# A four-layer graph network on one core: weights loaded by SP in the order of use, and the order of steps rearranged

## The chip, the cores and the metric

The kernel runs on one core of a Trainium2 chip. The metric is the device time of one execution in microseconds (us). Three runs of the kernel before are at hand, and one more execution that the hardware profiler recorded; all rows below come from that one.

## What is computed

64 independent graphs, each with 128 nodes and 384 features, pass through four stages, and each stage is added to the stream x of features:

```python
h = relu(layernorm(x)); x = x + L0(h, adj)   # "a": 2 layers; softmax(h h^T) * adj, three weights (left, self, right)
h = relu(layernorm(x)); x = x + L1(h, adj)   # "b": 2 layers; bilinear scores with two weights, one linear weight
h = relu(layernorm(x)); x = x + L2(h, adj)   # "c", layer 0: 12 heads, Wq, Wk, Wv, Wo
h = relu(layernorm(x)); x = x + L3(h, adj)   # "c", layer 1: 12 heads, Wq, Wk, Wv
```

There are 3 + 3 + 3 + 3 + 4 + 3 = 19 weights of 384 x 384, all used by every graph.

## The kernel before

**Numbers.** Products with weights run in float16 on TensorE (PE). Each weight is kept as two halves: `w_hi`, the weight times 64 rounded to float16, and `w_lo`, what the rounding lost. Activations are split the same way. A weight arrives in one of four stage buffers (`w_stage`: two of its own, and the still unused tiles `score` and `prob`), ScalarE (ACT) writes its upper half (`split_high`, L668), then VectorE (DVE) its lower half (`split_low`, L966; in a trace it shows under its helper's line L699). A stage buffer is free again when the lower half is written (`w_lo_split`).

**Order.** Every engine executes its instructions in the order written. That order is made by `woven`: the work of a graph is cut into steps, a letter stands for a stream of steps, and the string `ORDER[engine]` is one period. In each period each letter takes its stream one step on; `FIRST` says in which period and at which occurrence a stream begins. So graph g's stage a runs beside stage b of graph g - 1 and stage c of g - 2 and g - 3, and a steady period handles one graph's worth of everything. On PE: `a` turns the node features (transposes through the unit matrix), makes the scores of stage a (called U here), turns the attention, and makes the context (ctx); `w` are its weight products, each in two steps, called hl, hr and hs here; `d` turns the adjacency (L391, one instruction in each period, a handy mark); `b` and `x` are the same for stage b; `c` and `y` for stage c, whose turned features wait in bank c0, v product in c1, q and k in c2 and c3.

**Weights in the first periods.** SP loads the first four weights, after x and adj of two graphs and beta. The split of the first three weights stands ahead of everything else on ACT and DVE. The other 16 are put between steps at the places of `SPLITS` (period, place). Their loads are issued by ACT inside `split_high`: ahead of splitting weight m it waits for `w_lo_split` to reach m, and issues the load of weight m + 3. ACT also issues the two small copies that put the bias halves into `bias_hl`. POOL (GpSimd) begins with the memset of `bias_hl` (L1034) and then makes the constants; later it computes the inverse roots (`rstd`, L992). SP issues x and adj of graph g once `x1` of graph g - 2 is there (`load`).

**Names in the rows.** `node_a`, `node_b`, `node_c`: normalized features, whose turning on PE (L328) begins a layer; `hta_hi`, `hta_lo`: turned features of stage a; `sides`: copies of hl and hr; `self_part`: copy of hs times the diagonal of the attention; `ctx_a` (L766) adds it; `x1` is written at L792, x2 at L868 and L947.

## Time and profile before

| | us |
|---|---|
| median of 3 runs | 3139.33 |
| lowest and highest | 3137.36, 3139.83 |
| the profiled execution, its own time | 3139.59 |
| its span, first to last instruction | 3137.8 |
| busy in the span: PE, PE's weight loads (PEld) | 3032.1 (97%), 2337.5 (74%) |
| busy: DVE, ACT, POOL | 2606.3 (83%), 2094.4 (67%), 377.2 (12%) |
| granted PE clock, mean | 0.984 |

1.8 us of the profiled execution lie outside the span. A PE matmul is shown with its full latency, and the next one begins inside it, so the distance between two starts tells the pace, and a short pause can hide in a busy figure. Matmuls are counted as busy on PE, loading of the stationary operand on PEld. PEclk is the granted clock as a share of 2.4 GHz. "<-" behind an idle time names what ended it.

### The profile page before, as it was taken

Reading aid. Unit: us, or ns where it says so; the run is one execution under the profiler, and the core shown is the slowest. Engines: PE = TensorE matmul, PEld = TensorE weight load, DVE = VectorE, ACT = ScalarE, POOL = GpSimd, SP = SyncE. Lnnn points to the kernel's source line nnn. Section 1 sums busy time; section 2 is a strip of 40 time slices with the busy share of each in tenths; the row PEclk is TensorE's granted clock in tenths of the full one; section 3 lists DMA queues with packets and bytes.
Section 4 is the critical chain, followed back from the end, with each engine's and each line's share of the span. In section 5 each row is a group of like instructions: output and inputs, shape, how many; then the busy total and the mean of one; then the engine's idle time right before and its main releaser. Section 6 shows DMA issues by size and latency. Waiting matters only on the chain. (4 is left out here: it accounts for less than half of the span.)

```text
span 3137.8 us, 87682 instructions
## 1 busy us (share of the span) xinstructions
PE 3032.1 (97%) x34944; PEld 2337.5 (74%) x34944; DVE 2606.3 (83%) x7641; ACT 2094.4 (67%) x6037; POOL 377.2 (12%) x652
## 2 busy tenths in 40 slices
PE   3899999999999999999999999999999999999986
PEld 1677777777777777777777777777777777777764
DVE  4688888888888888888888888888888888888874
ACT  4467677677677677677676676676676666666664
POOL 1111111111111111111111111111111111111100
PEclk7999999999999999999999999999999999999996
DMA  5000000000000000000000000000000000000000
GB/s 174 4 14 11 10 13 11 12 12 11 13 10 11 13 10 11 13 10 11 13 10 11 14 10 11 13 10 11 14 10 11 13 10 11 14 10 11 10 7 6
DMA packets 37904, 47.82 MB, mean 15 GB/s; under 512 B 4542, under 2 KB 37498, under 8 KB 37498
## 3 DMA queue, kind: packets, MB, share of 16 engines
q1 hardware_dynamic: 31408, 33.31, 3.4%
q10 hardware_dynamic: 6090, 8.91, 0.9%
q8 instruction: 278, 4.55, 0.6%
q14 instruction: 128, 1.05, 0.1%
HBM read 29.59 MB, written 12.58 MB: 13 GB/s over the span
## 5 line engine op out<-in xcount | busy, mean ns | idle before, releaser
L638 ACT ACTIVATE prob<-score,neg_head_max 128x128 f32<-128x128 f32 x1536 | 494.1, 392 | 117.5 <-DVE neg_head_max L901 117.2
L284 PE MATMUL bank_c<-htc_hi,w_hi 128*128 128x128 f16 x2304 | 397.2, 220 | 0.0
L284 PE MATMUL bank_c<-htc_lo,w_hi 128*128 128x128 f16 x2304 | 397.1, 219 | 0.0
L284 PE MATMUL bank_c<-htc_hi,w_lo 128*128 128x128 f16 x2304 | 397.0, 219 | 0.0
L284 PE MATMUL bank_a<-w_hi,hta_hi 128*128 128x384 f16 x1152 | 379.6, 330 | 0.0
L284 PE MATMUL bank_a<-w_lo,hta_hi 128*128 128x384 f16 x1152 | 378.8, 329 | 0.0
L699 DVE SCALAR_TENSOR_TENSOR pt_lo<-bank_c,pt_hi 128x384 f16<-128x384 f32 x512 | 271.1, 550 | 74.3 <-ACT pt_hi L518 70.1
L896 DVE SCALAR_TENSOR_TENSOR score<-bank_c,bias 128x384 f32<-128x384 f32 x512 | 281.0, 549 | 33.7 <-PE bank_c L459 29.8
L901 DVE TENSOR_REDUCE neg_head_max<-score 128x3 f32<-128x384 f32 x512 | 280.4, 548 | 6.8
L518 ACT ACTIVATE pt_hi<-bank_c 128x384 f16<-128x384 f32 x512 | 233.0, 481 | 63.5 <-PE bank_c L328 63.5
L328 PE MATMUL bank_c<-ident,prob 128*128 128x128 f32 x1536 | 257.8, 278 | 14.1 <-ACT prob L638 13.7
L284 PE MATMUL bank_a<-w_hi,hta_lo 128*128 128x384 f16 x1152 | 252.5, 329 | 0.0
L328 PEld LDWEIGHTS bank_c<-ident,prob 128*128 128x128 f32 x1536 | 189.6, 143 | 75.7 <-issue 22.3
L284 PEld LDWEIGHTS bank_c<-htc_lo,w_hi 128*128 128x128 f16 x2304 | 226.0, 98 | 9.3 <-issue 0.3
L284 PEld LDWEIGHTS bank_c<-htc_hi,w_hi 128*128 128x128 f16 x2304 | 226.0, 98 | 8.6 <-issue 0.5
L284 PEld LDWEIGHTS bank_c<-htc_hi,w_lo 128*128 128x128 f16 x2304 | 225.9, 98 | 0.0
L518 ACT ACTIVATE m_hi<-bank_b 128x384 f16<-128x384 f32 x256 | 125.1, 489 | 142.3 <-PE bank_b L322 126.7
L284 PE MATMUL bank_b<-htb_lo,w_hi 128*128 128x128 f16 x1152 | 209.4, 219 | 0.0
L284 PE MATMUL bank_b<-htb_hi,w_hi 128*128 128x128 f16 x1152 | 209.4, 219 | 0.0
L284 PE MATMUL bank_b<-htb_hi,w_lo 128*128 128x128 f16 x1152 | 209.4, 219 | 0.0
L284 PE MATMUL bank_a<-sides,attn_ta 128*128 128x384 f32 x512 | 188.1, 490 | 2.8 <-DVE attn_ta L753 2.6
L284 PE MATMUL bank_c<-w_lo,htc_hi 128*128 128x384 f16 x576 | 190.0, 331 | 0.0
(200 smaller groups left out, 9183.0 us busy)
## 6 DMA issues: line engine op xcount, KB each, us to landing
x_in<-x SPq DMA_DIRECT2D x64, 192.0 KB, 2.4
out<-y_out SPq DMA_DIRECT2D x64, 192.0 KB, 1.9
w_stage<-w_t ACTq DMA_DIRECT2D x8, 576.0 KB, 3.9
adj_in<-adj SPq DMA_DIRECT2D x64, 64.0 KB, 2.1
score<-w_t ACTq DMA_DIRECT2D x4, 576.0 KB, 4.0
prob<-w_t ACTq DMA_DIRECT2D x3, 576.0 KB, 4.0
norms<-norm_rows SPq DMA_DIRECT2D x8, 192.0 KB, 6.3
w_stage<-w_t SPq DMA_DIRECT2D x2, 576.0 KB, 6.3
```

The lines of the kernel that those rows point to most:

```text
L284: mm = nc.tensor.matmul(out_ap, a, b, start=first and i == 0, stop=last and i == len(pairs_of) - 1)
L328: mm = nc.tensor.transpose(bank[:, c * 128:(c + 1) * 128], src(c), ident[:, :])
L518: return nc.scalar.activation(dst, src, ACT.Copy, scale=scale)
L638: ex = nc.scalar.activation(prob[:, j, c, :], score[:, j, c, :], ACT.Exp, bias=neg_head_max[:, j, c:c + 1])
L699: return V.scalar_tensor_tensor(dst, src, scale, hi, op0=ALU.mult, op1=ALU.subtract)
L896: V.scalar_tensor_tensor(score[:, j, :, :], chunked(c_banks[j][:, 0:D]), scale, bias[:, :].unsqueeze(1).to_broadcast([128, CHUNKS, 128]), ...
L901: V.tensor_reduce(neg_head_max[:, j, :], score[:, j, :, :], AX.X, ALU.max, negate=True)\
```

## The change

The weights lie in the order of use (in stage a left, right, self; in stage c v, q, k). SP issues all 19 loads; each but the first four waits for the lower half of the weight that held its buffer, and between them SP issues the copies into `bias_hl`, the norm rows in three lots and beta. The loads of x of graph 2 and later stand behind all of this on SP, behind the last weight and six loads of `qk_bias`. No split stands ahead of the streams any more: all 19 have a place in `SPLITS`. PE waits for each weight by itself. POOL makes its constants before it clears `bias_hl`. The strings of `ORDER` and the starts in `FIRST` are new.

```diff
--- before.py
+++ after.py
@@ -13,28 +13,27 @@
 MASKED = -9.0e15
 W_INDEX = (0, 3, 6, 9, 12, 16)
 W_STAGES = 4
-W_FIRST = 3
 
 
 ORDER = {
-    "pe": "yyybacbwwwwcwacwcbacxxcccxcxxxcxayybxxwwcabyybyyyyyydbwcwxxxxaxwcxcacxccwcccxbcxyyyyya",
-    "act": "ccxaqcbacwcwncppcpbpbwpbammmxbmcwibiiacniccbnjjjwcbcpccpppbwjncb",
-    "dve": "abcabccbcbcabccbcaapzppbpzazpabapabapaaaapbbpibxbcabibbiabbabcjbamcccjcccajaccbappppbapaaa"
-           "abncbbanqcpbax",
-    "pool": "qacmabbnab",
+    "pe": "xyyybyaybyayywcwwwbwcacwcacccxxccxxxcxxyyabxxawbcwbyyyyyyyydbwcwxwxxcxxacxxwcccacccbxc",
+    "act": "cnbxcbaccawccwcppcpbpwnbpbqammmbxmibiciawcinccbjnjjwccpbccpppbwj",
+    "dve": "nbacaccaccncczcapapazppzbpabapabaapabapbipbbxabcibibbbacbmjbcccccajcaccabjqapapppbapababaa"
+           "cbbaxbcabpbabb",
+    "pool": "babqnacamb",
 }
 FIRST = {
-    "pe": {"a": (0, 3), "b": (1, 6), "c": (2, 20), "d": (1, 0), "w": (0, 6), "x": (1, 9), "y": (2, 13)},
-    "act": {"a": (1, 2), "b": (2, 6), "c": (3, 15), "i": (2, 0), "j": (3, 0), "m": (4, 0), "n": (0, 1), "p": (4, 0), "q": (4, 0), "w": (1, 3), "x": (3, 0)},
-    "dve": {"a": (1, 13), "b": (2, 19), "c": (3, 18), "i": (2, 0), "j": (3, 0), "m": (2, 0), "n": (0, 0), "p": (4, 0), "q": (3, 0), "x": (2, 1), "z": (4, 0)},
-    "pool": {"a": (1, 2), "b": (2, 2), "c": (4, 0), "m": (2, 0), "n": (0, 0), "q": (3, 0)},
+    "pe": {"a": (0, 4), "b": (1, 6), "c": (2, 20), "d": (1, 0), "w": (0, 6), "x": (1, 10), "y": (3, 0)},
+    "act": {"a": (1, 2), "b": (2, 7), "c": (4, 0), "i": (2, 0), "j": (3, 0), "m": (4, 0), "n": (0, 2), "p": (4, 0), "q": (3, 0), "w": (1, 3), "x": (3, 0)},
+    "dve": {"a": (0, 12), "b": (1, 14), "c": (2, 18), "i": (1, 0), "j": (2, 0), "m": (1, 0), "n": (0, 0), "p": (3, 0), "q": (2, 0), "x": (1, 1), "z": (3, 0)},
+    "pool": {"a": (1, 0), "b": (2, 1), "c": (3, 0), "m": (1, 0), "n": (0, 0), "q": (2, 0)},
 }
 
 SPLITS = {
-    "act": [(1, 39), (1, 48), (1, 48), (1, 61), (1, 61), (2, 3), (2, 7), (2, 9),
-            (2, 21), (2, 24), (2, 24), (2, 24), (2, 37), (2, 43), (2, 48), (2, 50)],
-    "dve": [(1, 59), (1, 64), (1, 79), (1, 87), (1, 92), (1, 97), (2, 0), (2, 17),
-            (2, 29), (2, 33), (2, 40), (2, 45), (2, 52), (2, 59), (2, 65), (2, 79)],
+    "act": [(0, -1), (0, 43), (1, 1), (1, 27), (1, 39), (1, 43), (1, 51), (1, 62),
+            (1, 62), (2, 6), (2, 9), (2, 10), (2, 13), (2, 22), (2, 22), (2, 27), (2, 40), (2, 46), (2, 48)],
+    "dve": [(0, -1), (0, 10), (0, 45), (0, 54), (0, 54), (0, 65), (0, 77), (0, 93),
+            (0, 97), (0, 101), (1, 4), (1, 7), (1, 19), (1, 40), (1, 45), (1, 50), (1, 59), (1, 65), (1, 77)],
 }
 
 
...
@@ -229,6 +228,8 @@
             order, first = ORDER[engine], FIRST[engine]
             assert set(order) == set(streams), (engine, set(order) ^ set(streams))
             live, period = set(streams), 0
+            for _ in range(SPLITS.get(engine, []).count((0, -1))):
+                next(splits)
             while live:
                 seen = dict.fromkeys(streams, 0)
                 for place, letter in enumerate(order):
...
@@ -256,18 +257,41 @@
                 sp.wait_ge(*y_ready.at(g))
                 sp.dma_start(out[g:g + 1, :, :].rearrange("a p d -> (a p) d"), y_out[g % 2][:, :]).then_inc(y_stored[g], 16)
 
+            def load_weight(m):
+                if m >= W_STAGES:
+                    sp.wait_ge(w_lo_split, m - W_STAGES + 1)
+                sp.dma_start(w_stage[m % W_STAGES], w_t[m, :, :].rearrange("(c p) n -> p c n", p=128))\
+                    .then_inc(w_loaded[m % W_STAGES], 16)
+
+            def load_norms(first, last):
+                for i in range(first, last):
+                    sp.dma_start(norms[:, i, :], norm_rows[i:i + 1, :].to_broadcast([128, D]))\
+                        .then_inc(norms0_loaded if i < 2 else norms_loaded, 16)
+
             load(0)
+            for m in range(W_STAGES):
+                load_weight(m)
             load(1)
+            load_norms(0, 2)
+            sp.wait_ge(bias_zeroed, 1)
+            sp.wait_ge(b_hi_split, 1)
+            sp.dma_start(bias_hl[0:1, :, :], b_hi).then_inc(b_spread, 16)
+            sp.wait_ge(b_lo_split, 1)
+            sp.dma_start(bias_hl[1:2, :, :], b_lo).then_inc(b_spread, 16)
+            load_weight(4)
+            load_norms(2, 4)
+            load_weight(5)
+            load_weight(6)
+            load_norms(4, 8)
+            load_weight(7)
             sp.dma_start(beta_col[:, :], beta[0:1, :].to_broadcast([128, 1])).then_inc(beta_loaded, 16)
-            for m in range(W_STAGES):
-                sp.dma_start(w_stage[m], w_t[m, :, :].rearrange("(c p) n -> p c n", p=128)).then_inc(w_loaded[m], 16)
+            for m in range(8, N_W):
+                load_weight(m)
             for i in range(2):
-                m = W_INDEX[5] + i
+                m = W_INDEX[5] + 1 + i
                 for c in range(CHUNKS):
                     sp.dma_start(qk_bias[:, i, c:c + 1], biases[m:m + 1, c * 128:(c + 1) * 128].rearrange("a p -> p a"))\
                         .then_inc(qk_bias_loaded, 16)
-            for i in range(8):
-                sp.dma_start(norms[:, i, :], norm_rows[i:i + 1, :].to_broadcast([128, D])).then_inc(norms_loaded, 16)
             for g in range(2, graphs):
                 load(g)
                 if g >= 4:
@@ -372,16 +396,17 @@
                     yield
                     rows_rest(a0, m, hta_hi, hta_lo, None).then_inc(hl_done[g], 1)
                     yield
+                    weights(g, l, 1)
+                    pe.wait_ge(*expo_a_ready.at(g, k))
+                    rows_first(a1, m + 1, hta_hi)
+                    yield
+                    rows_rest(a1, m + 1, hta_hi, hta_lo, None).then_inc(hr_done[g], 1)
+                    yield
+                    pe.wait_ge(*hl_ready.at(g, k))
                     weights(g, l, 2)
-                    pe.wait_ge(*expo_a_ready.at(g, k))
-                    rows_first(a1, m + 2, hta_hi)
-                    yield
-                    rows_rest(a1, m + 2, hta_hi, hta_lo, None).then_inc(hr_done[g], 1)
-                    yield
-                    pe.wait_ge(*hl_ready.at(g, k))
-                    rows_first(a0, m + 1, hta_hi)
-                    yield
-                    rows_rest(a0, m + 1, hta_hi, hta_lo, None).then_inc(hs_done[g], 1)
+                    rows_first(a0, m + 2, hta_hi)
+                    yield
+                    rows_rest(a0, m + 2, hta_hi, hta_lo, None).then_inc(hs_done[g], 1)
                     yield
 
             def turn_adj(g):
...
@@ -486,13 +512,14 @@
             def weight_c(g):
                 for l in range(2):
                     k, m = l + 1, W_INDEX[4 + l]
-                    weights(g, 4 + l, 3 - l)
+                    weights(g, 4 + l, 0)
                     pe.wait_ge(*htc_hi_ready.at(g, k))
-                    rows_first(c1, m + 2, htc_hi)
-                    yield
-                    rows_rest(c1, m + 2, htc_hi, htc_lo, htc_lo_ready.at(g, k)).then_inc(v_done[g], 1)
-                    yield
-                    for bank, of, done in (c2, 0, q_done), (c3, 1, k_done):
+                    rows_first(c1, m, htc_hi)
+                    yield
+                    rows_rest(c1, m, htc_hi, htc_lo, htc_lo_ready.at(g, k)).then_inc(v_done[g], 1)
+                    yield
+                    for bank, of, done in (c2, 1, q_done), (c3, 2, k_done):
+                        weights(g, 4 + l, of)
                         for o in range(CHUNKS):
                             mm = columns(bank, m + of, htc_hi, htc_lo, o)
                             if o == CHUNKS - 1:
...
@@ -659,29 +687,17 @@
                         yield
 
             def split_high(m):
-                n = m + W_STAGES - 1
-                if W_STAGES <= n < N_W:
-                    act.wait_ge(w_lo_split, m)
-                    act.dma_start(w_stage[n % W_STAGES], w_t[n, :, :].rearrange("(c p) n -> p c n", p=128))\
-                        .then_inc(w_loaded[n % W_STAGES], 16)
                 act.wait_ge(w_loaded[m % W_STAGES], 16 * (m // W_STAGES + 1))
                 nc.scalar.activation(w_hi[:, m, :, :], w_stage[m % W_STAGES], ACT.Copy, scale=W_SCALE).then_inc(w_hi_split, 1)
 
             def later_weights():
-                for m in range(W_FIRST, N_W):
+                for m in range(N_W):
                     split_high(m)
                     yield
 
             act.dma_start(b_rows, biases[:, :]).then_inc(b_loaded, 16)
             act.wait_ge(b_loaded, 16)
             nc.scalar.activation(b_hi, b_rows, ACT.Copy, scale=W_SCALE).then_inc(b_hi_split, 1)
-            act.wait_ge(bias_zeroed, 1)
-            act.wait_ge(b_hi_split, 1)
-            act.dma_start(bias_hl[0:1, :, :], b_hi).then_inc(b_spread, 16)
-            act.wait_ge(b_lo_split, 1)
-            act.dma_start(bias_hl[1:2, :, :], b_lo).then_inc(b_spread, 16)
-            for m in range(W_FIRST):
-                split_high(m)
 
             def stream(steps):
                 for g in range(graphs):
...
@@ -966,14 +982,12 @@
                 lo_part(w_lo[:, m, :, :], w_stage[m % W_STAGES], w_hi[:, m, :, :], W_SCALE).then_inc(w_lo_split, 1)
 
             def later_weights():
-                for m in range(W_FIRST, N_W):
+                for m in range(N_W):
                     split_low(m)
                     yield
 
             dve.wait_ge(b_hi_split, 1)
             lo_part(b_lo, b_rows, b_hi, W_SCALE).then_inc(b_lo_split, 1)
-            for m in range(W_FIRST):
-                split_low(m)
 
             def stream(steps):
                 for g in range(graphs):
@@ -1031,7 +1045,6 @@
                 inverse_root("c", g)
                 yield
 
-            P.memset(bias_hl[:, :, :], 0.0).then_inc(bias_zeroed, 1)
             P.memset(ident[:, :], 0.0).then_inc(consts_set, 1)
             P.memset(upper_lower[:, :, :], 1.0).then_inc(consts_set, 1)
             P.memset(upper_incl[:, :], 1.0).then_inc(consts_set, 1)
...
@@ -1042,6 +1055,7 @@
                                    (upper_incl[:, :], 1, ALU.is_ge)):
                 P.affine_select(out=tile, in_=tile, compare_op=op, fill=0.0, base=0,
                                 pattern=[[sign, 128]], channel_multiplier=-sign).then_inc(consts_ready, 1)
+            P.memset(bias_hl[:, :, :], 0.0).then_inc(bias_zeroed, 1)
             pool.wait_ge(consts_ready, 4)
             pool.wait_ge(dve_consts, 2)
 
```

The parts left out: PE waits by weight in `weight_b` too, DVE waits for the norm rows of its layer, and the host stacks weights and biases in the new order.

## Rows read from the trace of the kernel before

**Rows 1.** Source line L391: min/median/max ns, first and last start in us.

```profile
L391 PE MATMUL bank_b<-ident,adj_in x64: 273/279/280, 69.7 to 3028.5; 128*128 128x128 f32 x64
```

**Rows 2.** Windows: length; busy us of PE, PEld, DVE, ACT, POOL; PEclk; DMA share.

```profile
69.69:115.48 45.79, 34.18 (x258) 22.11 (x256) 26.12 (x76) 18.95 (x47) 4.35 (x7) 0.85 0.09 30
...
1000.00:1046.94 46.94, 46.74 (x547) 36.28 (x546) 40.21 (x120) 32.33 (x95) 5.76 (x11) 1.00 0.04 12
```

**Rows 3.** Timeline, 0 to 22 us: start, length, engine, line, [idle before <-releaser].

```profile
0.78 6.50 POOL L1034 MEMSET bias_hl<- 128x7680 f16 x1 [0.29 <-POOLq L1087]
...
3.24 0.96 SPq L263 DMA_DIRECT2D w_stage<-w_t  x2
...
5.95 4.25 SPq L267 DMA_DIRECT2D qk_bias<-biases  x6
...
9.04 1.16 ACT L668 ACTIVATE w_hi<-w_stage 128x1152 f16<-128x1152 f32 x1 [5.78 <-DMA w_stage<-w_t]
...
16.19 0.51 ACT L528 ACTIVATE spent_in<-x_in 128x384 f32<-128x384 f32 x1
...
19.73 0.90 PE L328 MATMUL bank_a<-ident,node_a 128*128 128x128 f32 x3 [19.73 <-ACT node_a L523]
```

**Rows 4.** Timeline of PE from 20 to 45 us.

```profile
21.90 0.48 PE L284 MATMUL bank_a<-bias_hl,ones 128*128 128x384 f16 x1 [1.26 <-DVE hta_lo L702]
...
24.97 0.33 PE L284 MATMUL bank_a<-hta_hi 128*128 128x128 f16 x3
...
44.77 0.90 PE L328 MATMUL bank_a<-ident,node_a 128*128 128x128 f32 x3 [7.25 <-DVE node_a L784]
```

**Rows 5.** Timeline of DVE from 37 to 45 us.

```profile
38.26 0.62 DVE L766 SCALAR_TENSOR_TENSOR ctx_a<-bank_a,r_den_a,self_part 128x384 f32<-128x384 f32 x1 [2.65 <-ACT self_part L586]
...
42.82 1.36 DVE L699 SCALAR_TENSOR_TENSOR w_lo<-prob,w_hi 128x1152 f16<-128x1152 f32 x1 [0.78 <-ACT w_hi L668]
```

**Rows 6.** Waits of ACT from 9 to 80 us: in total, times, longest.

```profile
ACT w_hi L668 <- DVE w_lo L699: 15.0, 9, 2.3
```

**Rows 7.** Waits of DVE from 44.77 to 67.6 us.

```profile
DVE w_lo L699 <- ACT w_hi L668: 7.5, 5, 2.5
```

**Rows 8.** Timeline from 67 to 76 us.

```profile
67.07 0.54 DVE L792 SCALAR_TENSOR_TENSOR x<-affine_a,x_in 128x384 f32<-128x384 f32 x1
...
67.64 0.33 SPq L248 DMA_DIRECT2D x_in<-x  x1
...
75.04 0.90 PE L328 MATMUL bank_b<-ident,node_b 128*128 128x128 f32 x3 [5.08 <-ACT node_b L523]
```

**Rows 9.** DMA issues: size, median us from issue to landing.

```profile
x_in<-x SPq DMA_DIRECT2D x64, 192.0 KB, 2.4
...
w_stage<-w_t ACTq DMA_DIRECT2D x8, 576.0 KB, 3.9
```

**Rows 10.** Timeline of PE in one steady period, at two places.

```profile
1497.28 0.22 PE L284 MATMUL bank_a<-hta_lo,hta_hi 128*128 128x128 f16 x1
1497.33 0.22 PE L284 MATMUL bank_a<-hta_hi,hta_lo 128*128 128x128 f16 x1
1497.56 0.39 PE L459 MATMUL bank_c<-qk 32*128 32x128 f32 x4
...
1510.22 0.22 PE L284 MATMUL bank_b<-htb_hi,w_lo 128*128 128x128 f16 x1
1510.40 0.33 PE L328 MATMUL bank_c<-ident,head_out 128*128 128x128 f32 x1
```

**Rows 11.** Timeline of DVE in the same period.

```profile
1488.98 0.62 DVE L766 SCALAR_TENSOR_TENSOR ctx_a<-bank_a,r_den_a,self_part 128x384 f32<-128x384 f32 x1 [0.19 <-ACT self_part L586]
...
1493.38 0.61 DVE L784 SCALAR_TENSOR_TENSOR node_a<-scaled_a,rstd_a,norms 128x384 f32<-128x384 f32 x1
...
1513.44 0.56 DVE L947 SCALAR_TENSOR_TENSOR x<-bank_c,x 128x384 f32<-128x384 f32 x1 [0.15 <-PE bank_c L284]
```

**Rows 12.** Timeline of PEld at the end of that stretch.

```profile
1518.11 0.31 PEld L328 LDWEIGHTS bank_c<-ident,node_c 128*128 128x128 f32 x3 [0.52 <-ACT node_c L523]
```

20 lines of the change are left out of this document (11 added, 9 removed).

## The prediction

> **What bounds the kernel now.** I read the windows first. In a steady period of 46.94 us PE is busy for 46.74 and DVE for 40.21 [rows 2]: the kernel is bound by the amount of work on PE, which the change leaves as it is. Then the mark L391, one instruction in each period: the first at 69.7 us, the last at 3028.5 [rows 1]. So the profiled span of 3137.8 us is 69.7 of filling, 63 periods of 46.97 on average, and 109.3 of emptying. The stretch between the first two marks is as long as a period though PE has only 258 of 547 instructions in it, at a granted clock of 0.85 [rows 2]: it is bound by the chain of one graph through the engines, not by work. The emptying stage is such a chain too (graph 63 alone). The change can gain in the 115 us up to the second mark, and gain or lose in the 61 steady periods, where 0.1 us a period is 6 us.
>
> **The change part by part.** I take the span of the profiled execution and add up by how much the turning of `node_b` of graph 0, now at 75.04 us [rows 8], comes earlier. All that follows hangs on it.
>
> *Up to the first turning, 19.73 us [rows 3].* ACT first splits three weights; the first waits 5.78 us for its load, which SP issued at 3.24, and the features are touched at 16.19, whence it takes 3.54 us to PE [rows 3]. After: the load is issued 3 SP instructions earlier, at about 1.7. With 3.9 us to land, as single loads have [rows 9], it is there at 5.6, with 5.8 us, as here, at 7.5. Then one upper half (1.16), the chain of 3.54, and within it two more upper halves of 1.16: 11.4 to 13.4. POOL's clearing of `bias_hl`, 6.50 us [rows 3], now starts at about 2.4 and ends at 9, before its first root is asked for at about 10. I take 12.2: **-7.5 us** (bounds -8.3 and -6.3).
>
> *From there to the second layer's turning, 44.77 [rows 4], 25.0 us.* Three things leave this chain. Hl was computed ahead of U, from 21.90 to 24.97 [rows 4], 3.1 us; now U is first. Hs came behind ctx, so that `ctx_a` waited 2.65 us for `self_part` [rows 5]; now hs is first. And between `ctx_a` at 38.26 and the turning at 44.77 lie 6.5 us with two lower halves, of which 42.82 is one, 1.36 long after a wait of 0.78 [rows 5]; the new order has none between, 3 us are left, and 3.5 go. Sum -9.25; more splits stand earlier in the chain, I keep **-9.0**. From below: -5.5, if the end of the chain takes 5.0 us as in the steady period (1488.98 to the end of `node_a`, 1493.99 [rows 11]) and one lower half of 1.36 and a wait of 0.6 come back earlier.
>
> *From there to x1, 67.07 [rows 8], 22.3 us.* Here DVE stands idle 7.5 us for upper halves, five times [rows 7], and ACT in turn 15.0 us for lower halves over the first 80 us [rows 6]. The reason is the old `split_high`: ACT waits for a lower half only to issue a load, and everything behind it in its queue waits too, then DVE for ACT. With the loads on SP this wait is SP's, and an upper half is ready ahead of its turn as long as its load is: SP may issue weight m once lower half m - 4 is done, four splits ahead, 3.9 us to land [rows 9], against some 3 us from one split to the next. Of the 7.5 I take **-5.7**, since part of it hid other waits (bounds -3 and -7.5).
>
> *From there to the turning of `node_b`, 8.0 us [rows 8].* `x1` moves ahead of a lower half and `shift` of "ab" too; one upper half now stands ahead of `node_b`: -1.36 x 2 + 1.16 = **-1.5**.
>
> *The load of x of graph 2.* Before, SP issued it right behind x1 (67.64 [rows 8]), being free. Now it stands behind the last weight, which waits for the fifteenth lower half, about 3.5 us after x1, and behind six loads of `qk_bias`, which took 4.25 us to issue [rows 3]; then 2.4 to land [rows 9]: some 10.5 us after x1. But ACT comes to the first reading of it right after `node_b`, 6.5 to 7 us after x1, and behind it are `htb_hi` of graph 0 and with it the whole of stage b; DVE's `htb_lo` is late next. So ACT stands about 3.5 to 4 us; PE meanwhile has hr of graph 1 (about 3 us at the slow clock), but the chain that bounds this stretch does not. I take **+3.0** (bounds 0, if PE's work covers it, and +5.5).
>
> Sum: -7.5 - 9.0 - 5.7 - 1.5 + 3.0 = **-20.7 us**; with the bounds taken as independent, -14 to -25.
>
> The Trainium skill (DMA: Bandwidth & Descriptors, "Issuing engines are not separate DMA queues") says that loads from all engines end on the same 16 DMA engines, and that another issuer saves only the sequencer's time. Taken alone it speaks against the size of my third term; the sum by it would be that of rival D. What it leaves out of account are the waits in front of the issues, which the trace shows on ACT.
>
> *The emptying, 109.3 us.* In both orders the last period of PE holds all of stage c of graph 63 and nothing else, behind the same turning. One reduction (`head_min`) moves ahead of the last maximum, which only the fourth part of the heads feels. I take 0.
>
> *The steady periods.* Three pauses of PE show now. Between U and the scores 0.23 us instead of 0.05, waiting for k [rows 10]: another step now stands between, the pause goes, -0.17. Ahead of the turning of `head_out` 0.18 [rows 10]: it moves 0.17 us of PE work closer to what it waits for, +0.17 at worst. Ahead of the turning of `node_c` PEld waits 0.52 us [rows 12]; that chain takes 4.7 us from DVE's x2 (1513.44 [rows 11]) on; 0.13 us more work covers it: -0.1. The turning of `node_a` (second layer) now has 6.3 us of PE work between ctx and itself instead of 8.9 (the steps between, at 0.055 us for 128 columns [rows 10] and three times that for 384). Its chain is 5.0 [rows 11] plus `attn_b`, about 5.6: just covered. The sum of -0.1 is smaller than what DVE's new order may do to it; I take 0, with -0.25 to +0.25 a period, times 61: **0** (-15 to +15). Hidden by this full PE are also the split loads and all small waits past the second mark.
>
> Span 3137.8 - 20.7 = 3117.1; with 1.8 outside 3118.9; the profiled execution (3139.59) is 0.3 above the median of 3139.33. Prediction **3119 us**.
>
> **The rivals.**
>
> A. *The steady order gets worse, at `node_a`.* Its queue on DVE now has `htc_lo`, `delta_b` and `attn_b` in front, and `delta_b` waits for ACT's `expo_b`; if that comes late, PE waits for the turning in each period. For it: the cover sinks by 2.6 us to within 0.7 of the need. Against: PE shows no wait at this place now, and 0.7 us is more than one DVE instruction of this size (0.56 to 0.62 [rows 11]). From 0.34 us a period on (20.7/61) the change loses; with 0.5 it is 3119 + 30 = 3149.
>
> B. *The steady order gets better*: the pauses of k and `node_c` go and none comes, -0.2 x 61: 3107.
>
> C. *The gain is given back before the second mark*: once graph 1 is in, PE's own work at a clock of 0.85 (34.2 us busy of 45.8 [rows 2]) and the late x take half of it. -10: 3129.
>
> D. *The moved loads change nothing but their place*: DVE and ACT must still do 19 splits of 1.36 and 1.16 us within the same chain, and waits for upper halves become waits for PE. What stays is ACT's time for 15 issues, 0.48 us each (two in 0.96 [rows 3]), 7 us, of which the late x takes some 4: 3136. For it: each of the 19 splits still passes through both queues. Against: the 7.5 and 15.0 us of waits [rows 6, 7].
>
> **How the numbers follow.** Forecast (3119, from -14 to -25) 0.48, B 0.14, C 0.19, D 0.07, A 0.12. A measurement of this kernel tells apart 0.2%, 6.3 us. Faster are the forecast, B and C, 0.81; the same is D with a little of A, 0.08; slower the rest of A, 0.11. The range goes from B with a better filling, 3102, to just past D, 3137, leaving out some 0.04 below and 0.13 above. The likeliest case alone: 3111 to 3127.
>
> **What would show it.** First turning of `node_a` at 11.4 to 13.4 us; the second at 26 to 31; first L391 mark 18 to 26 us earlier than 69.7; no wait of ACT's `w_hi` for `w_lo`, but for DMA if SP is late; a wait of ACT on the load of x of 3 to 5 us right behind `node_b`; second mark near 95; distance of marks in the steady part 46.9 +- 0.25; 109 us from the last mark to the end. Wrong it goes if the steady distance moves by more than that, or if the second mark moves by less than 14 us.

## The result, and the profile after

| | before | after |
|---|---|---|
| median, us | 3138.57 (4 runs) | 3062.78 (4 runs, 3061.55 to 3064.76) |
| profiled span | 3137.8 | 3061.6 |

The ratio is 0.9759, 95% interval 0.9742 to 0.9776. That is 2.4% faster, 56 us below the forecast of 3119 and outside its range of 3102 to 3137.

First the marks. In the new file L391 has become L416. Source line L416 of the kernel after; the columns are those of [rows 1]:

```profile
L416 PE MATMUL bank_b<-ident,adj_in x64: 272/278/421, 46.0 to 2955.2; 128*128 128x128 f32 x64
```

Windows of the kernel after: from the first mark to the second, to the third, one steady period, and from the last mark to the end.

```profile
46.00:86.77 40.77, 33.73 (x256) 23.02 (x255) 24.69 (x74) 16.37 (x39) 4.68 (x7) 0.82 0.16 42
86.77:131.79 45.02, 43.19 (x477) 33.40 (x474) 36.81 (x114) 28.15 (x81) 7.98 (x13) 1.00 0.03 8
...
1000.00:1046.28 46.28, 46.28 (x548) 36.45 (x547) 40.76 (x119) 31.96 (x95) 6.31 (x10) 1.00 0.04 12
2955.19:3061.60 106.41, 72.68 (x818) 54.10 (x815) 60.84 (x140) 51.52 (x146) 3.96 (x7) 0.76 0.02 7
```

The span shrank by 76.2 us, in four pieces. Up to the second mark, 115.48 before [rows 2] and 86.77 now: 28.7 us. The next interval, 47.65 before: 2.6 us. The 61 periods behind it: from 2865.4 us (3028.51 less 163.13) to 2823.4, so 42.0 us, or 0.69 a period; the median of the distances fell from 46.94 to 46.28, 0.66. The emptying: 2.9 us. More than half lies where the forecast put nothing.

The filling stage, PE's timeline. The first row is the first turning, the second that of the second layer, the third the first mark, the fourth the turning of `node_b`:

```profile
11.86 0.90 PE L352 MATMUL bank_a<-ident,node_a 128*128 128x128 f32 x3 [11.86 <-ACT node_a L551]
...
27.49 0.90 PE L352 MATMUL bank_a<-ident,node_a 128*128 128x128 f32 x3 [4.38 <-DVE node_a L800]
...
46.00 0.42 PE L416 MATMUL bank_b<-ident,adj_in 128*128 128x128 f32 x1
48.44 0.90 PE L352 MATMUL bank_b<-ident,node_b 128*128 128x128 f32 x3 [2.01 <-ACT node_b L551]
```

These answer to 19.73, 44.77, 69.69 and 75.04 of before [rows 2 to 4, 8]. SP and ACT around the late load, and ACT's waits from 9 to 80 us:

```profile
46.81 2.86 SPq L293 DMA_DIRECT2D qk_bias<-biases  x6
...
49.71 0.43 SPq L249 DMA_DIRECT2D x_in<-x  x1
54.18 0.52 ACT L556 ACTIVATE spent_in<-x_in 128x384 f32<-128x384 f32 x1 [5.80 <-DMA x_in<-x]
```

```profile
ACT spent_in L556 <- DMA x_in<-x: 5.8, 1, 5.8
...
ACT w_hi L691 <- DMA prob<-w_t: 2.8, 1, 2.8
...
ACT w_hi L691 <- DMA score<-w_t: 2.1, 3, 1.6
```

The 15.0 us that ACT waited for lower halves [rows 6] are gone; what is left of `w_hi` waits for loads. The load of x comes late as forecast, and ACT stands 5.8 us for it.

The steady period. Waits of PEld from 1000 to 2000 us (some 21 periods), the kernel before and then the kernel after; PE itself has no wait there after:

```profile
PEld bank_c L328 <- ACT node_c L523: 11.5, 22, 0.8
...
PEld bank_a L284 <- DVE hta_lo L702: 9.2, 21, 0.5
```

```profile
PEld bank_c L485 <- issue: 13.6, 43, 0.3
PEld bank_b L436 <- DVE attn_b L847: 5.8, 22, 0.3
```

The two pauses of before, each about half a microsecond a period on PEld, are not there after. VectorE around them, the kernel before and then after, each with its stretch of one period:

```profile
1513.11 0.17 DVE L708 BATCH_NORM_AGGREGATE mean_var_a<-stats_a 128x2 f32<-128x6 f32 x1
...
1513.91 0.14 DVE L713 TENSOR_SCALAR var_eps_a<-mean_var_a 128x1 f32<-128x1 f32 x1
...
1515.04 0.62 DVE L784 SCALAR_TENSOR_TENSOR affine_a<-scaled_a,rstd_a,norms 128x384 f32<-128x384 f32 x1 [0.45 <-POOL rstd_a L992]
1515.57 0.55 DVE L702 SCALAR_TENSOR_TENSOR hta_lo<-bank_a,hta_hi 128x384 f16<-128x384 f32 x1
1516.04 0.14 DVE L718 TENSOR_SCALAR var_eps_c<-squares_c 128x1 f32<-128x1 f32 x1
```

```profile
1462.51 0.17 DVE L724 BATCH_NORM_AGGREGATE mean_var_a<-stats_a 128x2 f32<-128x6 f32 x1
...
1463.32 0.14 DVE L729 TENSOR_SCALAR var_eps_a<-mean_var_a 128x1 f32<-128x1 f32 x1
...
1463.95 0.56 DVE L963 SCALAR_TENSOR_TENSOR x<-bank_c,x 128x384 f32<-128x384 f32 x1
1464.43 0.62 DVE L800 SCALAR_TENSOR_TENSOR affine_a<-scaled_a,rstd_a,norms 128x384 f32<-128x384 f32 x1
...
1465.60 0.55 DVE L718 SCALAR_TENSOR_TENSOR hta_lo<-bank_a,hta_hi 128x384 f16<-128x384 f32 x1
1466.28 0.15 DVE L734 TENSOR_SCALAR var_eps_c<-squares_c 128x1 f32<-128x1 f32 x1
```

Before, x2 (1513.44 [rows 11]) stands ahead of `var_eps_a`; the root on POOL is asked for late, `affine_a` waits 0.45 us for it, and `hta_lo` and `var_eps_c` behind it are late. From x2 to `var_eps_c` it takes 2.60 us. After, the variance is made ahead of x2, the root is there in time, and the same way takes 2.33 us.

From the timelines one can also read how far the start of each PE step lies from the start of the next. Half a product with a weight (one step of hl, hr, hs, v, Wo or the linear product, five matmuls onto 384 columns) mostly takes 0.812 us, so more than that is a pause, though the busy column counts it as work, or it is the cost of what stands behind: ahead of the scores such a step takes 0.906 us in both kernels. (mr is the second bilinear product of stage b.) Median over the steady periods:

| step on PE, what stands behind it before | before | after |
|---|---|---|
| second half of the linear product of stage b, ahead of hl | 1.044 | 0.812 |
| second half of hl, ahead of the turning of `node_c` | 1.100 | 0.812 |
| U, ahead of the scores | 0.674 | 0.502 |
| part of mr, ahead of the turning of `head_out` | 0.627 | 0.503 |
| second half of the product with Wo | 0.919 | 0.812 |
| four others that shrank by 0.05 to 0.08 each, together | | -0.26 |
| eight that grew by 0.03 to 0.10 each, together | | +0.56 |

With -0.03 over all the others the sum is -0.66. One of the eight is the first half of hl, which now stands ahead of the scores and takes 0.906 us instead of 0.813. So of the 0.17 us that U gained by leaving that place, 0.09 are paid by the step that took it.

### The profile page after: what moved, and what is told of

It is laid out like the page before. It is cut to its first block, busy times and chain, and to the rows that moved or that the text cites. A ratio compares the mean times of both kernels' runs of the same rounds, so it can differ in the third digit from the quotient of the medians.

```text
span 3061.6 us, 87700 instructions
## 1 busy us (share of the span) xinstructions
PE 2994.7 (98%) x34944; PEld 2345.0 (77%) x34944; DVE 2634.4 (86%) x7641; ACT 2072.8 (68%) x6037; POOL 411.7 (13%) x652
## 3 DMA queue, kind: packets, MB, share of 16 engines
q8 instruction: 278, 4.55, 0.6%
## 4 chain that ended last, share of the span: by engine, by line
PE 94%; issue 1%; DVE 1%; ACT 1%; POOL 0%; POOLq 0%; ACTq 0%
PE bank_a L308 28%; PE bank_c L308 23%; PE bank_b L308 19%; PE bank_c L352 7%; PE bank_b L339 4%; PE bank_c L485 4%; PE bank_b L346 2%; PE bank_c L500 1%; PE bank_b L352 1%; PE bank_a L352 1%; PE bank_c L501 1%; PE bank_c L502 1%; PE bank_a L384 1%; PE bank_b L436 1%; PE bank_b L416 0%
## 5 line engine op out<-in xcount | busy, mean ns | idle before, releaser
L308 PE MATMUL bank_c<-htc_hi,w_hi 128*128 128x128 f16 x2304 | 405.9, 219 | 0.0
L308 PE MATMUL bank_c<-htc_lo,w_hi 128*128 128x128 f16 x2304 | 405.8, 219 | 0.0
L308 PE MATMUL bank_c<-htc_hi,w_lo 128*128 128x128 f16 x2304 | 405.8, 219 | 0.0
L1006 POOL TENSOR_TENSOR rstd_a<-var_eps_a,minus_half 128x1 f32<-128x1 f32 x128 | 109.2, 853 | 1360.3 <-DVE var_eps_a L729 1360.3
L352 PE MATMUL bank_c<-ident,prob 128*128 128x128 f32 x1536 | 247.5, 277 | 14.6 <-ACT prob L666 14.3
L546 ACT ACTIVATE sides<-bank_a 128x384 f32<-128x384 f32 x256 | 124.3, 486 | 132.4 <-PE bank_a L308 132.3
L308 PE MATMUL bank_a<-sides,attn_ta 128*128 128x384 f32 x512 | 197.8, 509 | 0.1
```

The costliest lines, as they stand in the source:

```text
L308: mm = nc.tensor.matmul(out_ap, a, b, start=first and i == 0, stop=last and i == len(pairs_of) - 1)
L352: mm = nc.tensor.transpose(bank[:, c * 128:(c + 1) * 128], src(c), ident[:, :])
L546: return nc.scalar.activation(dst, src, ACT.Copy, scale=scale)
L1006: P.tensor_tensor(rstd[of][:, :], src, exponent[:, :], ALU.pow).then_inc(root_ready[of][g], 1)
```

## The experiments

Each edit is given on its base: the kernel after, unless the text says before. A line of `ORDER` is one engine's period; the letter that moved can be found by comparing the two lines.

### The two halves of the change

*Old order with the new loads.* `ORDER`, `FIRST` and `SPLITS` as before (19 places, the first three ahead of the streams), the loads by SP as after.

```diff
-    "pool": "babqnacamb",
+    "pool": "qacmabbnab",
...
-    "act": [(0, -1), (0, 43), (1, 1), (1, 27), (1, 39), (1, 43), (1, 51), (1, 62),
+    "act": [(0, -1), (0, -1), (0, -1), (1, 39), (1, 48), (1, 48), (1, 61), (1, 61), (2, 3), (2, 7), (2, 9),
```

> The changed kernel with the old strings of ORDER, the old FIRST and the old places of the splits (the first three ahead of everything on ACT and DVE). Loads by SP, weights in the order of use and single waits for weights stay. Theory 1, the order of steps alone sets the steady period: L416 marks 46.9 us apart as before, and only part of the filling's gain stays (ACT no longer waits for lower halves); 3125 to 3134 us. Theory 2, the steady gain comes from the loads or the new order of weights in memory: marks 46.3 us apart, about 3085 to 3095 us.

Measured: 3131.08 us, ratio 0.9978 (0.9969 to 0.9988). First mark 62.01, 7.7 us earlier than before; the median distance 46.94, as before. Of the 7.7 us, 5.4 are there at the first turning (14.36 against 19.73). ACT's timeline, the kernel before and then this run:

```profile
8.20 0.72 ACTq L682 DMA_DIRECT2D bias_hl<-pt_lo  x1
...
12.11 1.16 ACT L668 ACTIVATE w_hi<-w_stage 128x1152 f16<-128x1152 f32 x1 [1.91 <-DVE w_lo L699]
```

```profile
6.67 1.16 ACT L691 ACTIVATE w_hi<-w_stage 128x1152 f16<-128x1152 f32 x1 [3.42 <-DMA w_stage<-w_t]
```

Before, ACT issues the two copies into `bias_hl` behind POOL's clearing and is free for its first split at 8.92; here it starts at 6.67 instead of 9.04. The three splits then follow each other by 1.5 us instead of 3.0, since ACT no longer waits for a lower half between them.

*New order with the old loads.* The kernel before, with `ORDER` and `FIRST` of after and the places of the 16 later splits; the first three stand ahead of the streams, ACT issues the loads inside `split_high`, and one split of ACT is five places later.

```diff
-    "pool": "qacmabbnab",
+    "pool": "babqnacamb",
...
-    "act": [(1, 39), (1, 48), (1, 48), (1, 61), (1, 61), (2, 3), (2, 7), (2, 9),
+    "act": [(1, 27), (1, 39), (1, 43), (1, 51), (1, 62), (1, 62), (2, 6), (2, 9),
```

> The kernel before (loads issued by ACT inside split_high, first three splits ahead, old order of weights) with the new ORDER and FIRST and the new places of the other 16 splits, one of them on ACT put a few steps later so that its wait for the lower half can be met. Theory 1: marks 46.3 us apart, 2.9 us less in the emptying, filling between the two kernels: 3080 to 3092 us. Theory 2: marks 46.9 us apart, above 3120 us.

Measured: 3079.84 us, ratio 0.9815 (0.9801 to 0.9830). First mark 62.56, 7.1 us earlier than before; the median distance 46.28. So the distance goes with the order of steps alone, to the hundredth, and has nothing to do with who issues loads. At the first mark the two halves give 7.7 and 7.1 us, together 23.7: 8.9 us exist only with both. By stages, in us:

| stage | before | new loads, old order | old loads, new order | after |
|---|---|---|---|---|
| up to the first turning | 19.73 | 14.36 | 19.64 | 11.86 |
| to the second layer's | 25.04 | 23.37 | 17.78 | 15.63 |
| to x1 | 22.30 | 21.28 | 21.18 | 15.41 |
| to the turning of `node_b` | 7.97 | 9.74 | 10.35 | 5.54 |
| to the second mark | 40.44 | 39.02 | 33.21 | 38.33 |

ACT's waits from 9 to 80 us in the run with new order and old loads:

```profile
ACT w_hi L665 <- DVE w_lo L696: 25.9, 14, 3.8
ACT w_hi L665 <- issue: 5.5, 1, 5.5
```

The new order puts the splits earlier, so ACT, while it still has to issue loads, waits more for lower halves than before (25.9 us against 15.0 [rows 6]). With the old order and the new loads this wait is gone, but the splits stand in ACT's queue behind steps that wait for PE:

```profile
ACT sides L546 <- PE bank_a L308: 13.5, 6, 6.2
```

Either way VectorE stands for upper halves. Its waits for them from 9 to 76 us, in the order of the table's columns:

```profile
DVE w_lo L699 <- ACT w_hi L668: 24.2, 15, 6.4
```

```profile
DVE w_lo L715 <- ACT w_hi L691: 19.5, 12, 4.6
```

```profile
DVE w_lo L696 <- ACT w_hi L665: 19.5, 11, 6.1
```

```profile
DVE w_lo L715 <- ACT w_hi L691: 1.8, 3, 1.1
```

The run with the old loads also keeps POOL's clearing of `bias_hl` first, the three early splits and the old order of weights. No wait of PE for a split shows in it up to 76 us, but its first turning is as late as before; what share of the 8.9 us that has was not tested.

### The filling stage

*The load of x of graph 2 ahead of weight 17.*

```diff
             for m in range(8, N_W):
+                if m == 17:
+                    load(2)
                 load_weight(m)
...
-                load(g)
+                if g > 2:
+                    load(g)
```

> The changed kernel, but SP issues x and adj of graph 2 ahead of the load of weight 17 instead of behind all weights and the qk_bias loads. If the 5.8 us that ACT stands waiting for x of graph 2 are on the chain: no such wait, the second adjacency mark 3 us earlier, 3060 us. If PE's work covers it: same as the changed kernel, 3063 within 1 us.

Measured: 3057.97 us, ratio 0.9746 (0.9732 to 0.9761). Timeline and window of this run:

```profile
44.83 0.34 SPq L246 DMA_DIRECT2D x_in<-x  x1
...
50.49 0.51 ACT L556 ACTIVATE spent_in<-x_in 128x384 f32<-128x384 f32 x1
```

```profile
48.21:82.83 34.62, 30.46 (x256) 20.95 (x255) 24.27 (x72) 16.49 (x39) 4.35 (x7) 0.92 0.13 37
```

ACT no longer waits. The stretch between the first two marks is 6.15 us shorter than after (34.62 against 40.77); 3.3 of these are PE's own busy time (30.46 against 33.73), at a granted clock of 0.92 instead of 0.82. The first mark came 2.2 us later; some 0.9 of that is a load that landed later (ACT's wait for `prob` 3.7 instead of 2.8), the rest was not traced. The second is 3.9 us earlier. So the late load costs the kernel after some 4 to 5 us.

*The first three weights split ahead of all streams.* The loads stay with SP.

```diff
-    "act": [(0, -1), (0, 43), (1, 1), (1, 27), (1, 39), (1, 43), (1, 51), (1, 62),
+    "act": [(0, -1), (0, -1), (0, -1), (1, 27), (1, 39), (1, 43), (1, 51), (1, 62),
...
-    "dve": [(0, -1), (0, 10), (0, 45), (0, 54), (0, 54), (0, 65), (0, 77), (0, 93),
+    "dve": [(0, -1), (0, -1), (0, -1), (0, 54), (0, 54), (0, 65), (0, 77), (0, 93),
```

> The kernel after, with the first three weights split ahead of all streams on ScalarE and VectorE again; the loads stay with SP. Prediction's reasoning (two upper halves stood ahead of the first features): first turning 2 to 3 us later than 11.86, first mark 2 to 3 us later than 46.0, total 3064 to 3067 us. Rival (the splits are needed by the first layer anyway, so only their place changes): first turning later, but the first mark within 0.7 us of 46.0 and the total 3062 to 3064 us. The distance of marks stays 46.28 in both.

Measured: 3061.76 us (2 runs), ratio 0.9762 (0.9743 to 0.9782). PE's timeline:

```profile
14.90 0.91 PE L349 MATMUL bank_a<-ident,node_a 128*128 128x128 f32 x3 [14.90 <-ACT node_a L548]
29.25 0.55 PE L349 MATMUL bank_a<-ident,node_a 128*128 128x128 f32 x3 [3.30 <-DVE node_a L797]
...
46.31 0.42 PE L413 MATMUL bank_b<-ident,adj_in 128*128 128x128 f32 x1
```

The first turning is 3.0 us later, the second layer's 1.8, the first mark 0.3, and the second mark (86.14) 0.6 us earlier. The rival holds: the first layers need these splits anyway, and a faster first turning mostly moves them behind it.

*Both together.* The two edits above.

> The kernel AFTER with two things of the filling changed: x of graph 2 is loaded ahead of weight 17 (as in the run with that alone), and the first three weights are split ahead of all streams. Theory 1: the early x gives its 4 to 5 us again, the place of the first splits gives within 1 us, total 3056 to 3060 us, distance of marks 46.28. Rival (the two need each other's slack): the early x gives nothing here, 3061 to 3063 us.

Measured: 3059.22 us, ratio 0.9755 (0.9740 to 0.9769); first mark 46.14, second 81.72, distance 46.28. The early x gives 4.4 us at the second mark here too (against 86.14); against the run with the early x alone nothing can be told apart in the total.

### The steady period: taking parts out of the kernel after

*x2 ahead of the variance of `node_a`*, one VectorE step.

```diff
-    "dve": "nbacaccaccncczcapapazppzbpabapabaapabapbipbbxabcibibbbacbmjbcccccajcaccabjqapapppbapababaa"
+    "dve": "nbacaccaccncczcapapazppzbpabapabpaaabapbipbbxabcibibbbacbmjbcccccajcaccabjqapapppbapababaa"
```

> The changed kernel with one step of DVE moved in all periods: x2 of stage c (which waits for PE's Wo product) again ahead of var_eps_a and scaled_a, as in the old order. Theory A, that step ahead of var_eps_a delays POOL's rstd_a, so affine_a, hta_lo and the root of stage c come late and PE waits twice: pauses come back, marks 46.5 to 46.7 us apart, 3075 to 3088 us. Theory B, the pauses went because PE has other steps there now: 46.3, 3063 us.

Measured: one run, 3123.44 us; median distance 47.31, 1.03 us more. PE's wait from 1000 to 2000 us:

```profile
PE bank_b L433 <- DVE attn_b L844: 15.4, 21, 0.7
```

x2 waits for the product with Wo, and all behind it on VectorE waits with it. But most of what came is not the pause at `node_c`: 0.86 us stand ahead of the turning of the attention of stage b, some steps further on in VectorE's queue, and 0.17 ahead of hl. x2's place matters as expected, at over twice the price.

*The scores right behind k*: U two steps later, and one product behind the scores instead of ahead of them.

```diff
-    "pe": "xyyybyaybyayywcwwwbwcacwcacccxxccxxxcxxyyabxxawbcwbyyyyyyyydbwcwxwxxcxxacxxwcccacccbxc",
+    "pe": "xyyybyaybyyyacwwwwbwcacwcacccxxccxxxcxxyyabxxawbcwbyyyyyyyydbwcwxwxxcxxacxxwcccacccbxc",
```

> The kernel after, with two steps moved on TensorE: the step U goes ahead again to stand behind the first half of ... k as before, so that the scores of stage c follow the last part of k with U between, and one product with weights goes behind them. Theory 1 (the DVE order around x2 and affine_a sets most of the gain, the k pause a part of 0.17 us a period): the distance of marks rises from 46.28 by 0.1 to 0.2 us, 3069 to 3075 us. Rival (PE has spare cover or the pause only moves): 46.28 within 0.05, 3060 to 3066 us.

Measured: 3080.81 us, ratio 0.9823 (0.9808 to 0.9837); median distance 46.57. From U to the next step it takes 0.790 us instead of 0.502: the pause came back, with 0.29 us, larger than the 0.17 it had before, and above the 0.1 to 0.2 that I had expected.

*TensorE's steps from hl to the attention of b in the order of before.*

```diff
-    "pe": "xyyybyaybyayywcwwwbwcacwcacccxxccxxxcxxyyabxxawbcwbyyyyyyyydbwcwxwxxcxxacxxwcccacccbxc",
+    "pe": "xyyybyaybyayywcwwwbwcacwcacccxxccxxxcxxyyabxxwwcabbyyyyyyyydbwcwxwxxcxxacxxwcccacccbxc",
```

> The kernel after, with the steps of TensorE between the second linear product and the turning of node_c of stage c in the old order (hl, hl, turning of node_c, U, attention of b). This also puts hl ahead of U in the first graph. Theory 1 (VectorE's order decides the pace, TensorE's order of these steps does not): distance of marks within 0.1 of 46.28; second turning of node_a 2 to 3 us later than 27.5, and the total 3063 to 3070 us. Rival (TensorE's own order of these steps gives the cover): the pauses ahead of hl and of node_c come back, 0.2 to 0.5 us a period, 3075 to 3095 us.

Measured: 3116.84 us, ratio 0.9936 (0.9920 to 0.9953); median distance 47.06. PE's wait from 1000 to 2000 us:

```profile
PE bank_b L305 <- DVE attn_tb_lo L712: 14.6, 21, 0.7
```

The two pauses in question stayed away: the linear product ahead of hl and hl ahead of the turning of `node_c` both take 0.812 us, with the old order of these steps. But my edit left nothing between the turning of the attention of b and its product, where the kernel before has a product of stage c, so 0.81 us came at that place. With it the other engines have 0.78 us more in each period, which may be what hides the two pauses; so the run does not show that PE's order of these steps is without effect. In the filling, with hl ahead of U, the second turning came 3.1 us later (30.60 against 27.49), of which 0.4 are the first turning's: 2.7 us, near the 3.1 of the prediction.

*`ctx_a` late*: on VectorE `diag_a` behind the head outputs, `ctx_a` behind a middle half, its statistics one step later, as before. The thirteenth lower half stands six places later as well, at (1, 25) of `SPLITS`, which touches the filling alone.

```diff
-    "dve": "nbacaccaccncczcapapazppzbpabapabaapabapbipbbxabcibibbbacbmjbcccccajcaccabjqapapppbapababaa"
+    "dve": "nbacaccaccncczcapapzppzbpabapabaaapabapbipbbxabcibibbbacbmjbcccccajcaccabjqapapppbapababaa"
```

> The kernel AFTER with one part of VectorE's order undone: diag_a behind the head outputs, ctx_a behind the first middle half of stage b, its statistics one step later, as before; x2 stays behind the variance of node_a. Theory 1b: ctx_a comes about 1 us later, the variance is ready only after x2 could start, x2 is late by 0.5 us and with it node_c and attn_b; distance of marks from 46.28 up by 0.3 to 0.6, total 3080 to 3100 us. Rival (the place of ctx_a is covered in the new order): within 0.1 us a period, 3060 to 3070 us.

Measured: 3159.26 us, ratio 1.0074 (1.0057 to 1.0090), slower than before; median distance 47.83. Waits of PE, and of ACT, from 1000 to 2000 us:

```profile
PE bank_c L305 <- ACT htc_hi L543: 11.4, 21, 0.5
PE bank_b L433 <- DVE attn_b L844: 9.7, 21, 0.5
```

```profile
ACT self_part L611 <- DVE diag_a L774: 49.5, 21, 2.4
```

With `diag_a`, a 128x1 product on VectorE, placed a few steps later, ACT stands 2.4 us a period for it; the head outputs' upper half `htc_hi` stands behind it in ACT's queue, and PE waits for that ahead of the product with Wo. That chain was not in my expectation. The step ahead of the product with Wo grew by 0.71 us, that ahead of the turning of the attention of b by 0.58, the turning of `node_a` by 0.19: with smaller ones 1.55 us a period, for three moves together.

### The steady period: putting parts into the kernel before

*x2 alone behind the variance.* On the kernel before.

```diff
-    "dve": "abcabccbcbcabccbcaapzppbpzazpabapabapaaaapbbpibxbcabibbiabbabcjbamcccjcccajaccbappppbapaaa"
+    "dve": "abcabccbcbcabccbcaapzppbpzazpabapabaaapaapbbpibxbcabibbiabbabcjbamcccjcccajaccbappppbapaaa"
```

> The kernel BEFORE with its loads and its order, and a single step of VectorE moved: x2 of stage c goes behind the two steps that make the variance of node_a of the second layer, instead of ahead of them. Theory 1 (this place decides): the pauses of TensorE ahead of hl and ahead of the turning of node_c shrink, distance of marks from 46.94 down by 0.3 to 0.5 us, total 3107 to 3120 us. Rival (the pace comes from many small places in the new order, or x2 itself sits on the chain of node_c, so that moving it later makes that wait longer): less than 0.1 us a period gained, or a loss, 3132 us or more.

Measured: 3143.49 us, ratio 1.0019 (1.0010 to 1.0028); median distance 47.03. PEld's waits from 1000 to 2000 us:

```profile
PEld bank_c L325 <- ACT node_c L520: 19.0, 22, 1.1
```

The wait for `hta_lo` is gone, and the product ahead of hl takes 0.812 us. But hl ahead of the turning of `node_c` takes 1.437 us instead of 1.100: the variance itself is ready only when x2 could long have run, x2 starts 0.48 us later, and what the one chain wins the other loses. My theory that this one place decides fell.

*VectorE's whole stretch around it.* On the kernel before: also `diag_a`, `ctx_a` and its statistics earlier, and the triangle product ahead of `hta_lo`.

```diff
-    "dve": "abcabccbcbcabccbcaapzppbpzazpabapabapaaaapbbpibxbcabibbiabbabcjbamcccjcccajaccbappppbapaaa"
+    "dve": "abcabccbcbcabccbcaapazpapbpzzpabapabaapabapbpibxbcabibbiabbabcjbamcccjcccajaccbappppbapaaa"
```

> The kernel BEFORE (its loads, its order of TensorE, ScalarE and GpSimd), with VectorE's steps from the last reciprocal of stage a to u_sum of stage b in the new order: diag_a ahead of the head reductions, ctx_a and its statistics each one step earlier, x2 behind the variance of node_a, the triangle product ahead of hta_lo. Theory 1b (what failed in the run with x2 alone moved was that the variance itself came 1.1 us too late; both chains need the earlier ctx_a): the pauses ahead of hl (0.23) and ahead of the turning of node_c (0.29) both go, distance of marks from 46.94 to 46.4 to 46.6, total 3105 to 3120 us. Rival (TensorE's own new order is needed as well): one of the two pauses stays, less than 0.3 us a period gained, 3122 us or more.

Measured: 3123.35 us, ratio 0.9959 (0.9944 to 0.9974); median distance 46.70. PEld's waits:

```profile
PEld bank_c L325 <- ACT node_c L520: 10.5, 21, 0.8
```

One of the two pauses stays, as the rival said (1.076 us instead of 1.100). The one ahead of hl is gone, and that behind the product with Wo (0.11) too, while the step ahead of the turning of `head_out` grew by 0.13. `node_c` now starts 4.55 us behind the start of the second half of the product with Wo instead of 4.92, but PE, no longer held ahead of hl, comes earlier too.

*And one step of TensorE.* On top of that, the turning of `node_a` behind the product with Wo.

```diff
-    "pe": "yyybacbwwwwcwacwcbacxxcccxcxxxcxayybxxwwcabyybyyyyyydbwcwxxxxaxwcxcacxccwcccxbcxyyyyya",
+    "pe": "yyybacbwwwwcwacwcbacxxcccxcxxxcxyyabxxwwcabyybyyyyyydbwcwxxxxaxwcxcacxccwcccxbcxyyyyya",
```

> The run of the kernel before with VectorE's steps in the new order, and one step of TensorE moved as well: the turning of node_a (first layer of the next graph) goes behind the product with Wo instead of ahead of it, as in the kernel after. Theory 2 (each pause has its own cover: x2 waits for that product, and node_c needs some 5.3 us from there, where TensorE had 5.04 us of other work and gets 0.33 more): the pause of 0.29 us ahead of the turning of node_c goes, distance of marks from 46.70 to 46.4 to 46.5, total 3105 to 3112 us. Rival (the turning is only work moved, or hl now waits for its lower half): distance within 0.08 of 46.70, 3118 us or more.

Measured: 3124.26 us, ratio 0.9956 (0.9941 to 0.9971); median distance 46.73. PEld's waits:

```profile
PEld bank_c L325 <- ACT node_c L520: 6.1, 22, 0.5
...
PEld bank_c L281 <- ACT htc_hi L515: 5.3, 21, 0.3
```

The pause at `node_c` shrinks by 0.22 us, as expected from the 0.33 us of cover. But the turning had covered another wait, that of the product with Wo for `htc_hi`, and the step ahead of it grows from 0.502 to 0.746 us. The sum is nothing. In the kernel after, the turning of `head_out` stands one step earlier as well, and this wait does not show.

*And two more*, on top of both: U behind the first third of k, a product ahead of the scores. Here too the strings are compared with those of before.

```diff
-    "pe": "yyybacbwwwwcwacwcbacxxcccxcxxxcxyyabxxwwcabyybyyyyyydbwcwxxxxaxwcxcacxccwcccxbcxyyyyya",
+    "pe": "yayybwcbwwwcwacwcbacxxcccxcxxxcxyyabxxwwcabyybyyyyyydbwcwxxxxaxwcxcacxccwcccxbcxyyyyya",
```

> The same with two more steps of TensorE moved: U behind the first third of k, and a product with weights ahead of the scores of stage c, as in the kernel after. Theory 2: the pause ahead of these scores (0.17 us) goes, up to 0.3 us a period, distance of marks 46.1 to 46.3, total 3090 to 3100 us. Rival (U is then late for its softmax, or the pause moves to the next step): no gain over the run without it.

Measured: 3238.25 us, ratio 1.0324 (1.0307 to 1.0341); median distance 48.60. PE's waits:

```profile
PE bank_a L281 <- ACT hta_hi L565: 10.7, 21, 0.5
...
PE bank_a L281 <- DVE hta_lo L699: 5.3, 21, 0.3
```

U follows its own turning with one step between here, where the kernel after has three, and waits for both halves of the turned features. The run says nothing on the k pause; it shows what a step costs that is placed too close behind its source.

## Why the prediction was wrong

**The failed step is the steady periods: "The sum of -0.1 is smaller than what DVE's new order may do to it; I take 0, with -0.25 to +0.25 a period".** Measured are -0.66 a period, 42 us of the 76. The run with the old order and the one with the new order show that the order of steps causes all of it. The step failed in three ways.

- *The pauses were read off too low.* I had the three that show as gaps in PE's row [rows 10, 12] and saw PE busy for 46.74 of 46.94 us [rows 2]. Compared with a step of the same kind elsewhere in the period, the kernel before pauses 0.23 us ahead of hl, 0.29 ahead of `node_c`, 0.17 at k, 0.12 ahead of the turning of `head_out` and 0.11 behind the product with Wo. The first and the last of these are not in the prediction at all, though PEld waits for the first. And the fourth had the wrong sign: it was taken to grow by up to 0.17 us a period, and it went.
- *`node_c` was costed by PE's cover alone* (-0.1), that is, by the work that PE has while it waits. Its chain got shorter too: 0.27 us at `var_eps_c`, as the timelines of VectorE show, and in the median 4.41 us instead of 4.92 from the second half of the product with Wo to `node_c`. The pause of 0.29 us went.
- *The bounds of 0.25 a period had no row.* Moves of one to a few steps cost 0.29 (U), 0.78 (PE's steps up to the attention of b), 1.03 (x2) and 1.55 us (`diag_a` and `ctx_a`) a period in the runs, so an order can lose that much; what it can win is bounded by the pauses that it finds, 0.92 us in the five rows of the table. Rival B had the sign and two of the places, with a third of the size. A did not come: PE has no wait from 1000 to 2000 us. When x2 was put ahead, PE did wait for an `attn_b`, but for that of the second layer, ahead of its own turning and not at `node_a`.

What carries the gain is not one place. VectorE's stretch alone gave 0.24 us in the kernel before; the next step of TensorE moved 0.24 us from one wait to another. Taken out of the kernel after, each part costs as much as or more than the share that it could have in the gain. That the five pauses go because several engines' orders fit each other is what these runs suggest; no run builds the whole gain up step by step. How the last 0.4 us divide among the remaining moves stays open: the run that should have added the cover of k was built so that U waited. Nor was it tested why eight steps grew by 0.03 to 0.10 us each; no wait of PE shows at them, and for one of them, the step ahead of the scores, it is the place and not the order that costs (0.906 us in both kernels).

**The filling: size nearly right, mechanism in part.** Up to the turning of `node_b` the sum was -23.7, measured -26.6: first turning -7.9 (taken -7.5), second layer -9.4 (-9.0), to x1 -6.9 (-5.7; x1 at 42.90), to the turning -2.4 (-1.5). Of the first term, the text puts two more upper halves into the chain and the sum only one (5.6 + 1.16 + 3.54 + 1.16 is 11.5); the trace has the two and a chain of 4.60 us (7.26 to 11.86) instead of 3.54, so one is what they cost. The second term is the order's, as said: 7.3 of its 9.4 us come with the order alone.

The other two reasons are only half right. The three early splits that I counted against the first turning cost the first mark 0.3 us when put back. And the third term, 5.7 us for loads issued by SP, is 1.0 us with the loads alone (22.30 to 21.28): the rest comes only when the splits stand earlier as well, as VectorE's waits for upper halves show (24.2 us before, 19.5 with either half, 1.8 with both).

The loads and what goes with them (POOL's order, the weights in the order of use) gave 7.1 us alone, by the medians of runs timed side by side. That is near the 7 us of rival D, which counted ACT's time for issuing, but by luck: 5.4 of the 7.7 us at the first mark are won up to the first turning, where ACT's two issues of loads took 0.44 and 0.37 us and its two waits for lower halves 1.91 and 1.84. The Trainium skill ("DMA: Bandwidth & Descriptors", "Issuing engines are not separate DMA queues") says that another issuer saves only the sequencer's time. That time is this small here; what was won is the waits that stood in front of the issues, of which the sentence does not speak.

**The late x: right in place, small in size.** Forecast were 3.5 to 4 us of ACT's wait and +3.0 in the total; measured 5.8 and some 4 to 5. Yet the stretch from the turning of `node_b` to the second mark did not grow: 38.3 us against 40.4. Without the late load it is 32.2 us, and with the new order and the old loads 33.2, so the new order is worth another 7 to 8 us here, which I had not looked for. A part of it goes with the clock: in this run with the old loads 0.92 was granted over the stretch, before 0.86. That is why the second mark stands at 86.8 and not near 95.

**The emptying: taken 0, measured -2.9.** Whether that is the change's doing stays open; see the last section.

## What to carry to other kernels

On a queue that looks full, compare the distance between starts of a step with that of the same kind of step elsewhere; the difference is the pause, whatever the busy column says, and times the number of periods it is about what a new order can win (here 0.92 us a period stood there, and 0.66 came out). Compare steps that have the same kind of step behind them, since that can cost 0.09 us by itself. When the order of steps changes on all engines, do not take a sum of named pauses for the whole: cost each queue's chains again, or keep a range of what single misplaced steps cost (0.3 to 1.5 us a period here). Moving one step takes its cover from another wait, so look at what it covered where it stood.

## What the runs showed of the hardware

The emptying stage differs in length with the same number of matmuls, 818. It took 109.3 us before and 106.4 after; in the run that moved only x2 in the kernel before it took 106.6. Of the fifteen profiled executions three have 108.7 to 109.4 us (the kernel before, the old order with the new loads, and VectorE's stretch put into the kernel before), the others 106.3 to 107.3. Window of the run that moved only x2, from its last mark, and that of the kernel before:

```profile
3035.17:3141.80 106.63, 72.65 (x818) 53.61 (x815) 60.45 (x141) 51.13 (x147) 3.94 (x7) 0.77 0.02 7
```

```profile
3028.51:3137.80 109.29, 75.69 (x818) 55.53 (x815) 60.43 (x141) 51.14 (x147) 3.94 (x7) 0.75 0.02 7
```

VectorE and ACT are busy for the same time; PE for 3.0 us less, at a mean granted clock of 0.77 instead of 0.75. What decides it was not tried. There is one profile of each kernel, and the runs of the kernel before spread over 6 us (3134.6 to 3141.0), so it may differ between executions of one kernel too. In the filling, too, part of what the early x gained is the clock: 0.92 instead of 0.82 between the first two marks.

Loads of a weight (576 KB) took longer to land in the kernel after, where SP issues them: in the median 4.7 us into `w_stage`, 6.5 into `score` and 6.0 into `prob`, against 3.9 to 4.0 for those that ACT issued before [rows 9]. The four that SP issued in a row before took longest, 6.3, 7.8 and 9.8 us, and with SP as the issuer but the old order, in which the splits and so the loads lie further apart, it was 4.3, 5.4 and 4.1. This points to how close the loads follow each other rather than to the issuer; it was not tested by itself.

The best version measured is the kernel after with the early x: 3057.97 us, by medians 4.8 us below the kernel after. The two were not timed side by side, and their intervals overlap (0.9732 to 0.9761, 0.9742 to 0.9776); that it is faster rests on the marks, where the second comes 3.9 us earlier and the distances behind it agree (45.02 us the next, 46.28 in the median).
